# Twelve expert blocks of the second half stand between the steps of the first group's second pass, and that group's B product stays in SBUF

## What is computed

```python
h = patch_embedding(x)                       # 32 x 38 x 192
h = h + ssm0(layernorm(h))                   # a scan over 16 states, forward
h = h + moe0(layernorm(h))                   # 8 experts, top 2 of 8, 192 -> 768 -> 192, gelu
h = h + up(mamba_f(down(layernorm(h))) + mamba_b(...reversed))   # two scans over 16 states
h = h + moe1(layernorm(h))                   # 8 experts, top 2, 192 -> 192
```

## Time and profile before

| | |
|---|---|
| time before, median of 3 runs | 993.15 us (992.44 to 998.41) |
| the profiled execution's own time | 998.04 us |
| its span, first to last instruction | 996.2 us |
| first pass with the blocks beside it | until about 345 us |
| blocks and the head of group 0 | 345 to 527 us |
| group 0, first scan to group 1's first scan | 534.5 to 621.6 us |
| groups 1, 2 and 3, first scan to last scan | 621.6 to 921.6 us |

### The profile page before, as it was taken

The page is one execution under the profiler, slowest core; times in us unless marked ns, Lnnn a source line. Parts: engine busy times, 40 slices in busy tenths (PEclk is TensorE's granted clock), DMA queues, the critical chain, the costliest instruction groups (busy, mean ns, idle before and its releaser), DMA issues.

```text
span 996.2 us, 11424 instructions
## 1 busy us (share of the span) xinstructions
PE 745.9 (75%) x3552; PEld 582.8 (58%) x3552; DVE 603.1 (61%) x993; ACT 406.2 (41%) x880; POOL 396.1 (40%) x311
## 2 busy tenths in 40 slices
PE   6978788784648798789995687758596868956746
PEld 5646556463438798779893465546374546643524
DVE  4177869778845324112125797898779687789220
ACT  2557283580323244223464444626262543442010
POOL 1156645854842322131002544453474326344403
PEclk8989798895868899999997788989799788976958
DMA  9569645543783678888848686855785549476011
GB/s 346 138 230 356 176 118 144 151 117 96 198 221 102 202 225 243 256 259 251 251 141 224 166 200 165 219 153 152 204 213 155 150 125 244 118 206 188 8 44 50
DMA packets 84668, 179.51 MB, mean 180 GB/s; under 512 B 12740, under 2 KB 32832, under 8 KB 83840
## 3 DMA queue, kind: packets, MB, share of 16 engines
q1 hardware_dynamic: 79776, 171.55, 61.1%
q0 software_dynamic: 4832, 7.24, 2.4%
HBM read 158.02 MB, written 20.69 MB: 179 GB/s over the span
## 4 chain that ended last, share of the span: by engine, by line
PE 28%; DVE 14%; issue 8%; DMA 6%; ACT 3%; SPq 3%; POOL 2%; POOLq 0%; DVEq 0%
PE PS L1630 27%; DVE ST L1297 4%; DMA BB<-rows_d 3%; DVE PS L1286 3%; DMA xp<-slots_d 2%; POOL PR L775 1%; POOL WX L783 1%; ACT dA L948 1%; ACT L899 1%; DVE p_WV L1353 0%; SPq L559 0%; PE PS L1842 0%; DVE m_Xr L1165 0%; SPq L546 0%; DMA rows_d<-p_WV 0%
## 5 line engine op out<-in xcount | busy, mean ns | idle before, releaser
L1630 PE MATMUL PS<-PR,CM 128*128 128x304 f32 (+1 forms) x672 | 189.9, 426 | 62.8 <-POOL PR L775 52.2
L775 POOL TENSOR_TENSOR PR<-ST,V 128x608 f32<-128x608 f32 x96 | 142.1, 1480 | 202.9 <-DVE ST L1297 152.4
L1630 PEld LDWEIGHTS PS<-PR,CM 128*128 128x128 f32 x672 | 131.4, 230 | 107.3 <-POOL PR L775 69.5
L948 ACT ACTIVATE dA<-dA,negA 128x304 f32<-128x304 f32 x192 | 94.0, 540 | 156.3 <-DMA BB<-rows_d 156.1
L1297 DVE TENSOR_TENSOR_SCAN ST<-dA,PS 128x608 f32<-128x608 f32 x96 | 136.4, 1420 | 12.7 <-ACT dA L948 5.3
L999 ACT ACTIVATE HID<-PS,WX 128x128 f32<-128x128 f32 x204 | 59.2, 367 | 134.4 <-PE PS L1630 132.1
L688 POOL TENSOR_TENSOR dA<-dA,aP 128x607 f32<-128x607 f32 x48 | 71.1, 1482 | 80.8 <-ACT aP L968 76.9
L1286 DVE TENSOR_TENSOR PS<-BB,PS 128x608 f32<-128x608 f32 x96 | 75.9, 791 | 20.6 <-DMA BB<-rows_d 16.2
L1485 DVE TENSOR_TENSOR xp<-PS,WXB 128x192 f32<-128x192 f32 x34 | 12.2, 358 | 124.4 <-PE PS L1630 124.4
L1630 PE MATMUL PS<-XT,WX 128*128 128x128 f32 x408 | 81.4, 282 | 1.1 <-ACT HID L999 1.0
L1630 PE MATMUL PS<-XT,WXR 128*128 128x128 f32 x408 | 80.9, 281 | 0.0
(11 more groups left out here) (322 smaller groups left out, 1331.3 us busy)
## 6 DMA issues: line engine op xcount, KB each, us to landing
dA<-rows_d SPq DMA_DIRECT2D x144, 304.0 KB
BB<-rows_d SPq DMA_DIRECT2D x144, 304.0 KB
...
```

The source lines that it names most:

```text
L775: nc.gpsimd.tensor_tensor(PRq[:, c % 2], STq[:, c % 2], DIRS[k].Cw.unsqueeze(1).broadcast_to([128, QB, T]), ALU.mult).then_inc(q_product.s ...
L948: last = nc.scalar.activation(dAq[:, slot, i, :], dAq[:, slot, i, :], ACT.Exp, scale=negA[:, j:j + 1])
L1630: return nc.tensor.matmul(out, lhsT, rhs, start=first, stop=last)
```

## The change

Blocks 15 to 19 stay in the preparation's part A (steps 0 to 4), 20 and 21 stand at steps 4 and 7 of its part B. Blocks 22 to 33 move behind steps of group 0's own second pass: behind steps 0, 2, 4, 6, 8, 10 of direction 0, and 0, 2, 4, 6, 8, 9 of direction 1 (the last `narrow` behind step 10). Every engine issues its part of a block at the end of that step. Group 0 needs only blocks 0 to 16. The wait for all stored blocks moves from the gather of group 1 to that of group 2.

To give the blocks PSUM banks, group 0's `b_product` writes its result back into the `BB` place of the ring, and its scan reads both operands from SBUF; groups 1 to 3 keep PSUM. Blocks 22 to 27 use banks 3 and 0, blocks 28 to 33 only bank 3, in the order first half of `widen`, `narrow(b - 1)`, second half, where the second half waits for the first three gelus. From block 17 on, the turned rows and results are in bank 6 instead of 7. Group 1's gathered rows get a buffer of their own (`GA1`). SP loads block 23 between `write_rows(0, 0)` and the first `read_rows`, and blocks 24 to 33 behind reads 4, 6, 8, ... 20 and 22 of group 0.

```diff
@@ -49,8 +49,14 @@
 IN_ROUTE = {0: 5, 1: 6, 2: 7, 4: 8, 5: 9, 7: 10, 8: 11, 9: 12, 10: 13, 11: 14}
-IN_PART_A = {0: 15, 1: 16, 2: 17, 3: 18, 4: 19, 5: 20, 6: 21, 8: 22, 9: 23, 10: 24, 11: 25}
-IN_PART_B = {0: 26, 1: 27, 2: 28, 3: 29, 4: 30, 5: 31, 6: 32, 7: 33, 8: 34}
+IN_PREP_A = {0: 15, 1: 16, 2: 17, 3: 18, 4: 19}
+IN_PREP_B = {4: 20, 7: 21}
+IN_FIRST_A = {0: 22, 2: 23, 4: 24, 6: 25, 8: 26, 10: 27}
+IN_FIRST_B = {0: 28, 2: 29, 4: 30, 6: 31, 8: 32, 9: 33, 10: 34}
+SPARE_BANK_BLOCKS = 28
+SLOT_OF = {b: half * QSTEPS + n for half, slots in enumerate((IN_FIRST_A, IN_FIRST_B)) for n, b in slots.items()}
+FIRST_BLOCK = min(SLOT_OF)
+LOAD_AT = {SLOT_OF[b - 2] + SLOTS: b for b in range(FIRST_BLOCK + 2, BLOCKS)}
 assert HALF_BLOCKS == 17 and SCAN_BLOCKS % 2 == 1
...
@@ -239,6 +245,7 @@
         XT = sb("XT", [128, 3, 2, 128])
+        GA1 = sb("GA1", [TW, TILES, 2, D])
 
...
@@ -248,11 +255,12 @@
         AS = (P.R, Q.R)
-        HX = HID[:, :, :].rearrange("p j t -> p (j t)")[:, 0:3 * FT * 128].rearrange("p (b f t) -> p b f t", f=FT, t=128)
+        HX = HID[:, :, :].rearrange("p j t -> p (j t)")[:, 10 * T - 3 * FT * 128:].rearrange("p (b f t) -> p b f t", f=FT, t=128)
         XB, YB = (xp[:, :, :].rearrange("p k t -> p (k t)")[:, j * 3 * D:(j + 1) * 3 * D].rearrange("p (b n) -> p b n", n=D)
...
         GA0 = BBK[0:TW, 0:2 * TILES * D].rearrange("p (t k n) -> p t k n", k=2, n=D)
+        GATHERED = (GA0, GA1[:, :, :, :], GA, GA)
         passed = xp[0:TW, :, :].rearrange("p k t -> p (k t)")[:, 6 * D:6 * D + 2 * HALF_BLOCKS * EXPERTS].rearrange("p (a b e) -> p a b e", a=2, e=EXPERTS)
...
@@ -399,11 +407,15 @@
 
-        SHARED_BANK = 7
+        def shared_bank(b):
+            return 7 if b < HALF_BLOCKS else 6
+
         HALF_FT = FT // 2
...
 
+            if b >= FIRST_BLOCK:
+                return ((3, 0) if b < SPARE_BANK_BLOCKS else (3, 3))[h]
             if b >= HALF_BLOCKS:
...
@@ -454,6 +466,15 @@
             return (IN_ROUTE if s is None else IN_SCAN).get(n)
+
+        def one_bank(b):
+            return 0 <= b < BLOCKS and wide_bank(b, 0) == wide_bank(b, 1)
+
+        def block_beside(g, nxt, half, n):
+
+            if nxt == 0:
+                return (IN_PREP_A, IN_PREP_B)[half].get(n)
+            return (IN_FIRST_A, IN_FIRST_B)[half].get(n) if g == 0 else None
 
...
@@ -634,17 +655,20 @@
             load_h(0)
-            for b in range(HALF_BLOCKS + 1, BLOCKS):
+            for b in range(HALF_BLOCKS + 1, FIRST_BLOCK + 1):
                 load_block(b)
-                if b == IN_PART_A[11] + 2:
+                if b == FIRST_BLOCK - 1:
                     load_next(0)
             write_rows(0, 0)
+            load_block(FIRST_BLOCK + 1)
             for g in range(GROUPS):
...
                     read_rows(g, 0, c)
+                    if g == 0 and c in LOAD_AT:
+                        load_block(LOAD_AT[c])
                     if c == 10 and g >= 2:
...
@@ -652,6 +676,8 @@
                     read_rows(g, 1, c)
+                    if g == 0 and QSTEPS + c in LOAD_AT:
+                        load_block(LOAD_AT[QSTEPS + c])
                     if c == 4:
...
@@ -761,7 +787,7 @@
                     for k in range(2):
-                        pool.indirect_dma_start((GA if g else GA0)[:, t, k, :], None, outs_d[g // PER_HALF][:, :],
+                        pool.indirect_dma_start(GATHERED[g][:, t, k, :], None, outs_d[g // PER_HALF][:, :],
                                                 bass.IndirectOffsetOnAxis(slot_u[:, t, k:k + 1], 0)).then_inc(gathered.sem, 16)
...
@@ -791,7 +817,7 @@
                         gather(0, range(TILES))
-                    if nxt == 1 and n == 4:
+                    if nxt == PER_HALF and n == 4:
                         rows_stored(every)
...
@@ -1283,7 +1313,7 @@
                 dve.wait_ge(q_scanned.sem, q_scanned.after(g, k * QSTEPS + c))
-                nc.vector.tensor_tensor(BPq[k], BBq[:, slot], BW[k].unsqueeze(1).broadcast_to([128, QB, T]),
+                nc.vector.tensor_tensor(BBq[:, slot] if is_first(g) else BPq[k], BBq[:, slot], BW[k].unsqueeze(1).broadcast_to([128, QB, T]),
                                         ALU.mult).then_inc(b_times_w.sem, 1)
...
@@ -1295,7 +1325,7 @@
                 nc.vector.tensor_tensor_scan(flat(STq[:, c % 2], back), flat(dAq[:, slot], back),
-                                             BP[k][:, ::-1] if back else BP[k], 0.0, ALU.mult, ALU.add).then_inc(q_scanned.sem, 1)
+                                             flat(BBq[:, slot] if is_first(g) else BPq[k], back), 0.0, ALU.mult, ALU.add).then_inc(q_scanned.sem, 1)
 
...
@@ -1899,7 +1938,7 @@
                     turn(b + 1)
-                if 0 <= b < SCAN_BLOCKS:
+                if one_bank(b):
                     widen(b, (0,))
...
@@ -2061,8 +2100,9 @@
                         mixture_rest(mix, n - 5)
-                    if nxt == 0 and n in IN_PART_A:
-                        experts(IN_PART_A[n])
+                    b = block_beside(g, nxt, 0, n)
+                    if b is not None:
+                        experts(b)
 
...
@@ -1859,6 +1891,13 @@
+                elif b == FIRST_BLOCK:
+                    pe.wait_ge(gelu_ready.sem, gelu_ready.after(b - 1, 2))
+                elif b > FIRST_BLOCK:
+                    if h and one_bank(b):
+                        pe.wait_ge(gelu_ready.sem, gelu_ready.after(b, 1))
+                    else:
+                        pe.wait_ge(gelu_ready.sem, gelu_ready.after(b - 1, 2 if h or one_bank(b - 1) else 1))
```

More of the change, by code:

```diff
@@ L811, in part_b @@
                         gate_inputs(tail, n - MIX_FROM)
-                    if nxt == 0 and n in IN_PART_B:
-                        store_block(IN_PART_B[n] - 1)
+                    b = block_beside(g, nxt, 1, n)
+                    if b is not None:
+                        store_block(b - 1)
             second_pass(pool, part_a, part_b)
@@ L1086, in part_a @@
                         squares(Q, tail, 0)
-                    if nxt == 0 and n in IN_PART_A:
-                        gelus(IN_PART_A[n])
+                    b = block_beside(g, nxt, 0, n)
+                    if b is not None:
+                        gelus(b)
             def part_b(g, tail, nxt):
@@ L1127, in part_b @@
                         step_logs(nxt, 0, None if g is None else (g, 1))
-                    if nxt == 0 and n in IN_PART_B:
-                        gelus(IN_PART_B[n])
+                    b = block_beside(g, nxt, 1, n)
+                    if b is not None:
+                        gelus(b)
             act.wait_ge(s_const[2], 32)
@@ L1484, in copy_y @@
                     dve.wait_ge(out_rows[p], 16 * (b // 3))
-                nc.vector.tensor_tensor(YB[:, p, :], PS[:, SHARED_BANK, 256:256 + D], WXB[:, p, :], ALU.add).then_inc(y_copied.sem, 1)
+                nc.vector.tensor_tensor(YB[:, p, :], PS[:, shared_bank(b), 256:256 + D], WXB[:, p, :], ALU.add).then_inc(y_copied.sem, 1)
             def copies(b):
@@ L1521, in combine @@
                 dve.wait_ge(gathered.sem, gathered.after(g, 16 * 2 * TILES))
-                rows = GA if g else GA0
+                rows = GATHERED[g]
                 for t in range(TILES):
@@ L1584, in part_a @@
                             centre(L, L, nxt, 0, L_BANK)
-                    if nxt == 0 and n in IN_PART_A:
-                        copies(IN_PART_A[n])
+                    b = block_beside(g, nxt, 0, n)
+                    if b is not None:
+                        copies(b)
             def part_b(g, tail, nxt):
@@ L1617, in part_b @@
                             output_norm(g, 0)
-                    if nxt == 0 and n in IN_PART_B:
-                        copies(IN_PART_B[n])
+                    b = block_beside(g, nxt, 1, n)
+                    if b is not None:
+                        copies(b)
             second_pass(dve, part_a, part_b)
@@ L1891, in narrow @@
                     pe.wait_ge(y_copied.sem, y_copied.after(b - 1, 1))
-                out = PS[:, SHARED_BANK, 256:256 + D]
+                out = PS[:, shared_bank(b), 256:256 + D]
                 for f in range(FT):
@@ L2104, in part_b @@
                         mixture(tail, n - MIX_FROM - 1)
-                    if nxt == 0 and n in IN_PART_B:
-                        experts(IN_PART_B[n])
-                    if nxt == 0 and n == QSTEPS - 1:
+                    b = block_beside(g, nxt, 1, n)
+                    if b is not None:
+                        experts(b)
+                    if g == 0 and n == QSTEPS - 1:
                         pe.wait_ge(y_copied.sem, y_copied.after(BLOCKS, 0))
```

10 lines of the change are left out of this document (5 added, 5 removed).

## The result

The changed kernel takes 1013.0 us (median of 4 runs, 1010.4 to 1017.1) against 995.8 us for the kernel before (992.4 to 1001.7, 4 runs). The ratio is 1.017, 95% interval 1.010 to 1.024: some 17 us **slower**, where 1011 was forecast. The profiled execution of the changed kernel took 1010.9 us, its span is 1009.1.

The account below looks back on a forecast made before the run. No engine was taken to bound the whole kernel; in the changed group 0 a DVE-PE-POOL loop would. First scan 38 us earlier, group 0 56 longer: +18 on 993.15, so 1011 us, range 988 to 1032.

Parts of the forecast that it names:

- The head: Last gather to group 0's first scan: 41 us from landing to `steps`; first scan at 496.4 instead of 534.5, 38 us earlier.
- Group 0: First scan of group 0 to group 1's: 143 us instead of 87.1, 56 us longer.
- the loop: Group 0, copy_y, B product, scan, POOL's product, sum, block: 10.3 us for two steps, 9.0 from block 28 on.
- The other work: Group 0's projections, `steps`, combine, gated output and norms, as far as waits don't swallow them: 23 us together.
- The second operand: Group 0's scans reading both operands from SBUF conflict with POOL's product: 1 to 3 us, inside the walk.
- the walk: Group 0, summed over fourteen stretches between ends of `narrow`, from start to group 1's first scan: 114.8 us before other work.
- it isn't the bound, the loop is: Check on PE in group 0: twelve blocks and other work make 111 of 143 us, so PE doesn't bind.
- transfers can begin to hold up steps: Check on DMA in group 0: 94 us of transfers in some 105, share 0.90; 0 to 15 us left in the range.
- (a): Rival: the loop doesn't close and group 0 is PE bound at 120 us; -5, or 982 with full-clock head; chance 0.13.
- (b): Rival: transfers in full (15 us) and half of the port's 13 us hold group 0; +38, 1031 us; chance 0.17.
- (c): Rival: about even, head 33 instead of 41 us, group 0 at 134; +2, 995 us; chance 0.22.
- (e): Rival: blocks don't overlap with group 0's steps at all, group 0 at 157 us; +32; chance 0.03.

Follow-up runs that it names:

- experiment 7: Changed kernel with block 23's five transfers issued behind the first step's reads instead of ahead of them: 1009.0 us, ratio 1.018 to the kernel before.
- experiment 6: Changed kernel with eight blocks moved instead of twelve, blocks 20 to 25 standing in the preparation: 1009.0 us, ratio 1.019 to the kernel before.
- experiment 1: Kernel before, blocks unmoved; only group 0's B product stays in the ring and its scan reads it there: 1000.6 us against 993.7, ratio 1.006.
- experiment 5: Changed kernel with copy_y and its store one step after the block's step, copy_x unmoved: 1009.7 us, ratio 1.017 to the kernel before.
- Experiments 2: Changed kernel where DVE copies and POOL stores block b - 2 instead of b - 1 in block b's step: 1004.8 us, ratio 1.013 to the kernel before.
- 3: Changed kernel loading only a quarter of the expert weights of blocks 24 to 33: 1020.0 us, ratio 1.028 to the kernel before.
- experiment 12: Kernel before with four blocks (30 to 33) moved into direction 0, B product in PSUM, copy_y one step later, early rows: 1002.8 us, ratio 1.012.

## Why the prediction was right, point by point

**The head** was forecast from the last gather's landing to the end of `steps` with 41 us and took 41.1 (435.84 to 476.96); from there to the first read 7.4, and it took 7.3. Two terms were mis-sized: the gather lands 5.8 us after its last issue, not 3.4, since behind the busy DVE of the kernel before the landing couldn't be seen; and from first read to first scan it is 10.6, not 9.5. Part of the second is a misreading: the read at 527.52 in the earlier trace rows is that of `BB`, and the first one, of `dA`, was issued at 526.91, so before it was 4.6 us from write to read and 7.6 from read to scan, not 5.2 and 7.0. So the head got 34 us shorter, not 38. The block that SP loads first entered the sum with 2.2 us of issuing (7.4 for 5.2) and 2.5 of waiting; taking it away gave 7.0, of which 5.6 lie in these two places (experiment 7). The lower clock is as forecast: projections 8.58 us (7.5 forecast), and it is the missing cover that lowers it (experiment 6).

**Group 0** was forecast with 143 us and took 142.1, the loop with 10.3 and 9.0; from copy_y to copy_y it took 10.3 (500.65 to 510.95) and 9.0 (558.18 to 567.15) where no other work stood in it, and 11.0 to 15.0 where it did. The other work was sized well too: five loops to block 27's took 57.5 us, 6.0 over the bare loops (5.8 forecast), and the next five 62.8, 17.8 over (17.3 forecast).

**The second operand** was forecast inside the walk with 1 to 3 us: seven scans there are longer by 3.3 us together. Alone it costs 4.1 in group 0 (experiment 1), and not the 16 of its upper bound.

**The step that failed** is a sentence of the checks, on PE: "it isn't the bound, the loop is". In size the loop was right; as a cause it is not alone. With the loop opened group 0 is 139.3, with transfers cut 144.4, with both 124.5, where PE is busy 109.2. So limits lay on top of each other: the loop at 142, transfers at 139, and at 125 what both leave, PE in direction 1 and a mixture of waits and lower clock in direction 0. The same holds for "transfers can begin to hold up steps": a share of 0.98 cost 2.2 us of waits ahead of decays and turns as long as the loop hid it, and about 15 once it didn't (12.2 and 3.4, experiment 5). Experiments 2, 3 and 5 were each expected to decide between them, and none could alone.

**The rivals.** (a), PE-bound with 120 in group 0, is nearly what remains when both others are taken away (124.5), and it doesn't come by itself. The sentence of the Trainium skill that interleaving regimes may help ("Perfetto Trace Analysis", section "Optimization Strategy") is not borne out by this case: PE's busy time in group 0 rises from 63 in 94 us (clock 0.80) to 113 in 142 us (0.91 and 0.95), and the time grows. (b) was too dear: the port isn't paid at every step, and the loop hides the transfers. (c) is some 17 us off. (e) would have had 157 in group 0.

**The balance**, from profiles: the head 34 us shorter, blocks in group 0 51 longer (142.1 - 91.2), the second operand 4, the stretches behind 2.6 less: +18. That it meets the forecast of +18 to the microsecond is luck: the head missed by 4, and group 0 by 1 and the stretches behind, which were put at nothing and here lie within the scatter of the traces, make up for it. In the preparation a block costs 99.0 - 64.9 = 34.1 by twelve, **2.9 us**; in group 0 50.9 by twelve, **4.2**. Alone it would be 5.8. In both places it hides part of its work behind something else, and in the preparation more. The price there isn't even: the first four taken out save 1.1 each (experiment 12), the next four 5.2 (94.6 to 73.8, though in another order), the last four 2.2 (experiment 6). The low first price has a reason in the traces: with the first blocks moved, a block's load stands ahead of the first reads. In experiment 12 write to read takes 8.4 us instead of 4.6 and read to scan 10.4 instead of 7.6, 6.6 more together; without them the first four would have saved 2.8 each.
